# Attention block of four 512-channel images on one core: batches written out one after the other, ScalarE sets the scores' starting values for every step, maxima in units of 256 and 512 keys

## The chip, the cores and the metric

The kernel runs on one core of a Trainium2 chip. The metric is the device time of one execution in microseconds (us). Before the change three runs gave 4076.78, 4077.01 and 4074.82 us, median 4076.78.

## What is computed

The reference is a group norm, eight-head attention over the 48 x 48 positions of an image, a projection, and the normalised input added back. Four images (batches) of 512 channels, T = 2304 positions, heads of 64 channels, all in fp32:

```
xn  = groupnorm(x, 32 groups) * gn_w + gn_b              # (4, 512, 2304)
q, k, v = split(qkv_w @ xn + qkv_b)                      # 8 heads of 64 channels
w   = softmax(q^T k / sqrt(64))                          # 2304 x 2304 per head
a   = v w^T
out = xn + proj_w @ a + proj_b
```

## The kernel before, in words

Two heads (a pair) are worked on together, each in one half of TensorE's 128 rows or columns. A batch has 4 pairs. A pair's queries are cut into 6 chunks of N = 384, its keys into 18 tiles of 128. A **step** is one key tile for one query chunk, both heads: scores of 128 keys x 384 queries per head, `Exp` on ScalarE (L756) into one of 8 ring places in `probs`, the product with the values on TensorE (`make_pv`, L577), and on GpSimd the addition into `denom` (L1087), 17 additions for the 18 steps of a chunk. Two steps make a **slot**; 9 slots make a block (one query chunk of a pair), 54 slots a pair, 216 slots a batch, 864 slots the kernel.

Before `Exp`, the scores must be lowered by each query's maximum. `max_unit` (L517) computes scores roughly, for 128 queries and one chunk of 384 keys, both heads, into `aux_banks`; VectorE takes the maximum of each (L864); when a block's queries are complete the maxima are negated (L869), transposed (L877), sent through DRAM (`neg_rows`) and read back over all partitions as `seeds`. This runs 24 steps ahead. The accurate scores of a step are three products (high parts, low part of keys, low part of queries, L557) added to the negated maximum already in the bank. In even steps ScalarE copies `seeds` into the bank (L769); in odd steps TensorE multiplies a matrix of 1/64 (`shares`) with `seeds` (L553).

TensorE's order inside a slot is written out:

```
unit_of_step(first); make_scores(first); make_scores(second); unit_of_step(second)
[pieces of projections of q, k, v for the next pair]   # before[i]
make_pv(first - 2); make_pv(first - 1)
[finish of a block: sum of denom over partitions]      # after[i]
```

There is one `aux_banks`: a unit waits until VectorE has taken the maxima of the unit before (`aux_done`). On ScalarE the order of a slot is `Exp`, `Exp`, seed of the next even step, then the high parts of q and k (L716), values (L720) or saving of the output sums (L741). VectorE takes the unit's maxima, pieces of the reciprocal of the sums (L945 to L961), and the low parts of q and k (L857), which wait for the high part. In the first three pairs of a batch (inner pairs) the projections for the next pair are cut into pieces: in each block three of them, and they end in slots 1, 5 and 8 of the block. Twelve of the eighteen in a pair are of q or k. In the last pair they are whole, and VectorE takes the next batch's statistics (slots 0 to 11), a short chain of small operations gives its coefficients (slots 14 to 16), and ScalarE normalises it (L736, slots 16 to 27).

When a batch's stream of slots ends, TensorE computes the last block's sums (L534) once GpSimd has finished, and then the projection (L656): six chunks of 384 positions, each 48 matmuls. Its input `att` is read back from DRAM into two buffers `att_in`, and split into a high part (ScalarE, L747, into the key buffers) and a low part (VectorE, L967, in place). ScalarE adds the bias into `proj_sb`, VectorE adds the normalised input to it in `xres` (L1022), both in the ring `probs`; SyncE stores `xres` and loads the input for the chunk after next into it. The next batch's first seed on ScalarE waits until the stores have landed. Every engine runs the first three batches as a loop (`Fori`), the fourth written out behind it.

Of the kernel before, what the change touches and what calls it, by code (L numbers as in the profile page):

```python
# [5 lines left out]
def attention_block_program(nc, x, gn_w, gn_b, wqkv_t, bqk, bv, wproj_t, bproj, att, out):  # L6
# [39 lines left out]
    AHEAD = KT + 6  # L46
    EARLY_Q = 2
# [13 lines left out]
    NORM_AT, NORM_EVERY = 33, 2  # L61

# [101 lines left out]
    with ExitStack() as ctx:  # L164
# [10 lines left out]
        seeds = [sb(f"seeds{i}", [128, 2 * N], fp32r) for i in range(2)]  # L175
        shares = sb("shares", [128, 128], fp32r)
# [15 lines left out]
        att_in = [sb(f"att_in{i}", [128, CT, N], fp32r) for i in range(2)]  # L192
# [3 lines left out]
        neg_max = sb("neg_max", [128, 32], fp32r)  # L196
# [3 lines left out]
        spare = sb("spare", [128, 1])  # L200
        small = sb("small", [128, 64])
# [12 lines left out]

        def head(e):
            return slice(e * D, (e + 1) * D)
# [9 lines left out]

        def xres(i):
            return probs[:, CT * N * i:CT * N * (i + 1)].rearrange("p (o n) -> p o n", n=N)

        proj_sb = probs[:, 2 * CT * N:4 * CT * N].rearrange("p (o n) -> p o n", n=N)  # L230
        att_hi = [buf[:, 0:CT * N].rearrange("p (k n) -> p k n", n=N)
                  for buf in (k_hi[(PAIRS - 1) % 2], k_lo[(PAIRS - 1) % 2])]
# [62 lines left out]
        def first_batch(k):  # L295
            return isinstance(k, int)
# [40 lines left out]
        def _(sp):  # L337
# [15 lines left out]
            def send_max(n, blk):  # L353
# [8 lines left out]
                if not isinstance(n, int) or n >= 2:  # L362
                    sp.wait_ge(seeded, PRIMED + KT // 2 * (n - 1))
                    sp.wait_ge(probs_ready, PROBS_PRIMED + KT * (n - 1))
                sp.dma_start(seeds[par][:, :].bitcast(fp32), neg_rows.rearrange("r q -> (r q)").partition_broadcast(128))\
# [8 lines left out]
            def stream(b, last):  # L374
                before, _ = PLANS[last]
                nb = b + 1
                for s in range(BSTEPS):
# [18 lines left out]
                    if s in PUT_AT:  # L396
                        put_block(b, PUT_AT[s])
# [13 lines left out]
            def load_att(b, tc):  # L411
                i = tc % 2
                sp.dma_start(att_in[i][:, :, :].bitcast(fp32), att[:, :, chunk(tc)]
                             .rearrange("k c t -> c k t")).then_inc(att_back[i], 16)
# [4 lines left out]
            def projection(b):  # L419
                sp.wait_ge(att_out, PRIMED + 16 * (BLOCKS * b + BLOCKS - 1))  # L420
                load_att(b, 0)
                load_att(b, 1)
                put_block(b, BLOCKS - 1)

                for tc in range(2):
                    if tc == 1:
                        sp.wait_ge(att_out, PRIMED + 16 * BLOCKS * (b + 1))
# [36 lines left out]
            with sp.Fori(0, B - 1) as b:  # L464
                batch(b, False)
            batch(B - 1, True)
# [11 lines left out]
        def _(pe):  # L478
            mm = nc.tensor.matmul

            def bank_for(u):

                if not isinstance(u[1], int) or u[1] > 0:
                    pe.wait_ge(bank_free[u[0]], u[1])
                return bank(u)
# [26 lines left out]
            def max_unit(n, p, qt, kc):  # L512

                if not isinstance(n, int) or n > 0:
# [23 lines left out]
            def make_scores(s, b):  # L538


# [4 lines left out]
                if s % 2 == 0:  # L545
                    pe.wait_ge(seeded, PRIMED + BSTEPS // 2 * b + s // 2 + 1)
                else:
                    if s >= 2:
                        pe.wait_ge(probs_ready, PROBS_PRIMED + BSTEPS * b + s - 1)
                    if kt == 1:  # L550
                        pe.wait_ge(seeds_in[blk % 2], 16 * (BLOCKS // 2 * b + blk // 2 + 1))
                    for e in range(2):
                        mm(slot[:, e, :], shares[head(e), :], seeds[blk % 2][head(e), e * N:(e + 1) * N],  # L553
                           start=True, stop=False)
                for n, (ks, qs) in enumerate(((k_hi[par], q_hi), (k_lo[par], q_hi), (k_hi[par], q_lo))):
                    for e in range(2):
                        last = mm(slot[:, e, :], ks[head(e), keys], qs[head(e), queries],  # L557
                                  start=False, stop=(n == 2), skip_group_check=(s % 2 == 0))
                last.then_inc(scores_full, 1)

            def open_banks():

                for e in range(2):
                    last = mm(scores[:, 0, e, 0:N], k_hi[0][head(e), 0:128], q_hi[head(e), chunk(0)],
                              start=True, stop=True)
# [53 lines left out]
            def stream(b, last):  # L619
# [17 lines left out]
                finish(b, BLOCKS - 1, use(b, last, TAIL))  # L637
                if not last:
                    wait_free(pe, use(b, last, ("v", PAIRS, VG - 1)))

            def projection(b):

                pe.wait_ge(wproj_lo_ready, 1)
                for tc in range(CH):
                    i = tc % 2
                    for low in range(2):
                        pe.wait_ge(att_lo_ready if low else att_hi_ready, CH * b + tc + 1)
                        products = ([(wproj_hi, att_in[i])] if low
                                    else [(wproj_hi, att_hi[i]), (wproj_lo, att_hi[i])])
                        for ot in range(CT):  # L650
# [3 lines left out]
                            for w, a in products:  # L654
                                for k in range(CT):
                                    last = mm(scores[:, n // 2 % 2, n % 2, 0:N], w[:, k, ot * 128:(ot + 1) * 128],  # L656
# [489 lines left out]
```

## Time and profile before

| | |
|---|---|
| median of three runs | 4076.78 us |
| profiled execution, device time | 4077.72 us |
| its span, first to last instruction | 4076.0 us |
| mean granted TensorE clock | 0.988 of full |
| TensorE busy | 3933.8 us, 97% |
| GpSimd busy | 3004.5 us, 74% |
| ScalarE busy | 2308.0 us, 57% |
| VectorE busy | 2217.9 us, 54% |

Busy is the time in which at least one instruction of the engine ran. TensorE's instructions overlap: two matmuls, one in each half of the array, start together, and the next two start before they have ended, so that the distance between starts and not the duration is what one costs. Shares are means over the whole span: the stream of slots, the last pair of a batch and the projection have to be read apart.

### The profile page before, as it was taken

Reading aid. Unit: us, or ns where it says so; the run is one execution under the profiler, and the core shown is the slowest. Engines: PE = TensorE matmul, PEld = TensorE weight load, DVE = VectorE, ACT = ScalarE, POOL = GpSimd, SP = SyncE. Lnnn points to the kernel's source line nnn. Section 1 sums busy time; section 2 is a strip of 40 time slices with the busy share of each in tenths; the row PEclk is TensorE's granted clock in tenths of the full one; section 3 lists DMA queues with packets and bytes.
Section 4 is the critical chain, followed back from the end, with each engine's and each line's share of the span. In section 5 each row is a group of like instructions: output and inputs, shape, how many; then the busy total and the mean of one; then the engine's idle time right before and its main releaser. Section 6 shows DMA issues by size and latency. Waiting matters only on the chain.

```text
span 4076.0 us, 84658 instructions
## 1 busy us (share of the span) xinstructions
PE 3933.8 (97%) x31730; PEld 2472.5 (61%) x31730; DVE 2217.9 (54%) x2809; ACT 2308.0 (57%) x3159; POOL 3004.5 (74%) x1639
## 2 busy tenths in 40 slices
PE   6999999999899999999989999999999999999997
PEld 3566665656656566565665656566567565656656
DVE  4555555565455555566545555556644555555552
ACT  2555555565455555556535555555654555555563
POOL 0778878777288888877728888887773888888893
PEclk9999999999999999999999999999999999999999
DMA  2000000120400000012130000002113000000004
GB/s 74 16 20 24 18 22 21 43 87 18 148 19 18 22 22 20 20 57 73 39 131 18 22 21 16 24 20 75 59 43 121 21 16 21 22 18 19 19 19 144
DMA packets 133751, 165.87 MB, mean 41 GB/s; under 512 B 61648, under 2 KB 110800, under 8 KB 132816
## 3 DMA queue, kind: packets, MB, share of 16 engines
q1 hardware_dynamic: 133328, 160.26, 12.5%
q8 instruction: 262, 4.29, 0.4%
q14 instruction: 161, 1.32, 0.1%
HBM read 122.17 MB, written 38.04 MB: 39 GB/s over the span
## 4 chain that ended last, share of the span: by engine, by line
PE 88%; issue 4%; DVE 3%; POOL 3%; DMA 2%; SPq 0%; ACT 0%; POOLq 0%; DVEq 0%; ACTq 0%
PE oacc L577 26%; PE scores L557 20%; PE pool_bank L495 13%; PE aux_banks L517 13%; PE pool_bank L507 7%; PE scores L656 3%; PE scores L553 3%; POOL denom L1087 3%; PE pool_bank L534 2%; DMA att_in<-att 1%; DVE maxima L864 1%; DVE turned L945 1%; DMA out<-probs 1%; PE scores L495 1%; PE scores L507 0%
## 5 line engine op out<-in xcount | busy, mean ns | idle before, releaser
L1087 POOL TENSOR_TENSOR denom<-denom,probs 128x768 f32<-128x768 f32 x1536 | 2829.3, 1842 | 568.3 <-ACT probs L756 473.3
L864 DVE TENSOR_REDUCE maxima<-aux_banks 128x2 f32<-128x768 f32 x1728 | 1657.2, 959 | 1389.1 <-PE aux_banks L517 1379.4
L756 ACT ACTIVATE probs<-scores 128x768 f32<-128x768 f32 x1728 | 1347.2, 812 | 1259.2 <-PE scores L557 1253.2
L577 PE MATMUL oacc<-probs,vals 128*64 128x384 f32 x6912 | 1277.0, 491 | 0.0
L517 PE MATMUL aux_banks<-k_hi,q_hi 64*128 64x384 f32 x3456 | 762.5, 437 | 43.2 <-DVE maxima L864 39.2
L577 PEld LDWEIGHTS oacc<-probs,vals 128*64 128x64 f32 x6912 | 471.1, 137 | 503.9 <-issue 466.8
L517 PEld LDWEIGHTS aux_banks<-k_hi,q_hi 64*128 64x128 f32 x3456 | 323.2, 184 | 693.2 <-issue 451.2
L769 ACT ACTIVATE scores<-seeds 128x768 f32<-128x768 f32 x864 | 700.1, 810 | 4.3 <-DMA out<-probs 4.3
L557 PE MATMUL scores<-q_hi,k_hi 64*128 64x384 f32 x3456 | 587.3, 335 | 22.7 <-ACT scores L769 22.6
L557 PE MATMUL scores<-q_lo,k_hi 64*128 64x384 f32 x3456 | 588.6, 335 | 0.0
L557 PE MATMUL scores<-q_hi,k_lo 64*128 64x384 f32 x3456 | 585.6, 334 | 0.0
L1084 POOL TENSOR_TENSOR denom<-probs 128x768 f32<-128x768 f32 x96 | 174.6, 1819 | 442.1 <-ACT probs L756 442.1
L557 PEld LDWEIGHTS scores<-q_hi,k_hi 64*128 64x128 f32 x3456 | 327.4, 186 | 33.9 <-ACT scores L769 32.7
L557 PEld LDWEIGHTS scores<-q_lo,k_hi 64*128 64x128 f32 x3456 | 328.0, 185 | 0.0
L557 PEld LDWEIGHTS scores<-q_hi,k_lo 64*128 64x128 f32 x3456 | 327.3, 185 | 0.0
L495 PE MATMUL pool_bank<-xn,wq 128*64 128x384 f32 x1504 | 293.2, 505 | 1.6
L553 PE MATMUL scores<-seeds,shares 64*128 64x384 f32 x1728 | 292.7, 334 | 0.0
L507 PE MATMUL pool_bank<-wv,xn 128*64 128x128 f32 x4416 | 287.9, 277 | 1.8
L495 PE MATMUL pool_bank<-xn,wk 128*64 128x384 f32 x1456 | 281.4, 501 | 1.9
L507 PEld LDWEIGHTS pool_bank<-wv,xn 128*64 128x64 f32 x4416 | 236.9, 137 | 42.9 <-issue 36.6
L553 PEld LDWEIGHTS scores<-seeds,shares 64*128 64x128 f32 x1728 | 163.2, 185 | 0.0
L495 PEld LDWEIGHTS pool_bank<-xn,wq 128*64 128x64 f32 x1504 | 90.1, 137 | 103.1 <-issue 96.8
(91 smaller groups left out, 1681.3 us busy)
## 6 DMA issues: line engine op xcount, KB each, us to landing
seeds<-neg_rows SPq DMA_DIRECT2D x96, 384.0 KB, 3.5
xtile<-x SPq DMA_DIRECT2D x72, 384.0 KB, 3.2
att<-o_norm SPq DMA_DIRECT2D x96, 192.0 KB, 1.9
att_in<-att SPq DMA_DIRECT2D x24, 768.0 KB, 6.3
probs<-x SPq DMA_DIRECT2D x24, 768.0 KB, 4.7
out<-probs SPq DMA_DIRECT2D x24, 768.0 KB, 5.2
neg_rows<-neg_cols SPq DMA_DIRECT2D x384, 0.8 KB
xn<-x SPq DMA_DIRECT2D x4, 1152.0 KB, 8.6
```

Of the source, the lines that this page charges most:

```text
L495: last = mm(to[head(e), 0:N], w[:, k, head(e)], xn[:, k, chunk(c)], start=(k == 0), stop=(k == CT - 1))
L507: last = mm(to[head(half), i * 128:(i + 1) * 128], xn[:, k, t0:t0 + D], wv[:, k, :], start=(k == 0), stop=(k == CT - 1))
L517: last = mm(aux_banks[:, e, 0:N], q_hi[head(e), qt * 128:(qt + 1) * 128], k_hi[p % 2][head(e), chunk(kc)], start=True, stop=True)
L553: mm(slot[:, e, :], shares[head(e), :], seeds[blk % 2][head(e), e * N:(e + 1) * N], start=True, stop=False)
L557: last = mm(slot[:, e, :], ks[head(e), keys], qs[head(e), queries], start=False, stop=(n == 2), skip_group_check=(s % 2 == 0))
L577: ins = mm(oacc[head(e), 0:N], vals[p % 2][:, kt, head(e)], prob(s)[:, e * N:(e + 1) * N], start=(kt == 0), stop=(kt == KT - 1))
L656: last = mm(scores[:, n // 2 % 2, n % 2, 0:N], w[:, k, ot * 128:(ot + 1) * 128], a[:, k, :], start=(not low and w is wproj_hi and k == 0), ...
L756: a(prob(s).rearrange("p (h n) -> p h n", n=N), scores[:, s % 2, :, 0:N], ACT.Exp, scale=SCALE).then_inc(probs_ready, 1)
L769: a(scores[:, 0, :, 0:N], seeds[blk % 2][:, :].bitcast(fp32).rearrange("p (e n) -> p e n", n=N), ACT.Copy).then_inc(seeded, 1)
L864: v.tensor_reduce(maxima[:, :, qt, kc], aux_banks[:, :, 0:N], AX.X, ALU.max).then_inc(aux_done, 1)
L1084: gp.tensor_tensor(acc, prob(s - 1), prob(s), ALU.add).then_inc(added, 1)
L1087: gp.tensor_tensor(acc, acc, prob(s), ALU.add).then_inc(added, 1)
```

## The change

Four things are changed.

1. The loops over batches are gone; each engine's program has all four batches one behind the other.
2. Seeds: ScalarE copies the negated maxima into the bank for all steps. Its order in a slot becomes `Exp(s)`, `seed(s+2)`, `Exp(s+1)`, `seed(s+3)`; a seed waits for the `Exp` just before it. TensorE's products with `shares` go.
3. Maxima units: the six units of 384 keys become three pairs of 256 and 512 keys. The unit at the head of a slot is of 256, the second of 512.
4. The end of a batch: the attention output has buffers of its own for raw, high and low part. The chunks 0 and 1 are loaded during block 20 and later of the last pair, chunk 2 after block 22; the high and low part of chunk 0 are made in four pieces in slots 43 to 47 of the last pair. The last block's sums are computed after the first chunk of the projection instead of ahead of it. `xres` and `proj_sb` change places in the ring, and wait for GpSimd accordingly. The next batch's seeds 0 and 1 are written by ScalarE between the last copies of the projection, and it waits for the stores only at step 4.

```diff
+    UNIT_KEYS = (256, 512)
+    SPLIT_AT = 43
-            with pe.Fori(0, B - 1) as b:
-                batch(b, False)
-            batch(B - 1, True)
+            for b in range(B):
+                batch(b, b == B - 1)
...
             def max_unit(n, p, qt, kc):
...
-                    last = mm(aux_banks[:, e, 0:N], q_hi[head(e), qt * 128:(qt + 1) * 128],
-                              k_hi[p % 2][head(e), chunk(kc)], start=True, stop=True)
+                    last = mm(aux_banks[:, e, 0:UNIT_KEYS[kc % 2]], q_hi[head(e), qt * 128:(qt + 1) * 128],
+                              k_hi[p % 2][head(e), unit_keys(kc)], start=True, stop=True)
...
             def make_scores(s, b):
-                if s % 2 == 0:
-                    pe.wait_ge(seeded, PRIMED + BSTEPS // 2 * b + s // 2 + 1)
-                else:
-                    if s >= 2:
-                        pe.wait_ge(probs_ready, PROBS_PRIMED + BSTEPS * b + s - 1)
-                    if kt == 1:
-                        pe.wait_ge(seeds_in[blk % 2], 16 * (BLOCKS // 2 * b + blk // 2 + 1))
-                    for e in range(2):
-                        mm(slot[:, e, :], shares[head(e), :], seeds[blk % 2][head(e), e * N:(e + 1) * N],
-                           start=True, stop=False)
+                pe.wait_ge(seeded, PRIMED + BSTEPS * b + s + 1)
...
                 make_pv(BSTEPS - 1, b, last)
-                finish(b, BLOCKS - 1, use(b, last, TAIL))
...
+            def projection(b, last):
                 for tc in range(CH):
+                    if tc == 1:
+                        finish(b, BLOCKS - 1, use(b, last, TAIL))
...
             def exponentials(s, b):
+                if s == 0:
+                    act.wait_ge(out_ready, PRIMED + PJ * b)
+                if s == RING // 2:
+                    for i in range(2):
+                        act.wait_ge(stored[i], PRIMED + 16 * (CH // 2) * b)
...
             def stream(b, last):                       # ScalarE
-                seed(0, b)
                 for i in range(PAIRS * SLOTS):
                     for s in range(GS * i, GS * i + GS):
                         exponentials(s, b)
-                    if GS * i + 2 < BSTEPS:
-                        seed(GS * i + 2, b)
+                        if s + 2 < BSTEPS:
+                            seed(s + 2, b)
...
+                    n = i - (PAIRS - 1) * SLOTS - SPLIT_AT
+                    if 0 <= n < CT:
+                        att_high(b, 0, slice(n, n + 1))
-                att_high(b, 0)
...
             def projection(b, last):                   # ScalarE
+                    if n == PJ - 3 and not last:
+                        seed(0, b + 1, PRIMED + PJ * b + n + 1)
+                    if n == PJ - 1 and not last:
+                        seed(1, b + 1, PRIMED + PJ * b + n + 1)
...
             def projection(b):                         # SyncE
-                    if tc + 2 < CH:
-                        sp.wait_ge(proj_full, PJ * b + CT * (tc + 1))
-                        load_att(b, tc + 2)
+                    if tc + 3 < CH:
+                        load_next_att(b, tc + 1)       # waits for att_lo_ready of chunk tc + 1
```

## Rows read from the trace of the kernel before

**Rows 1.** The page's chain that ended last, shares of the span by engine

```profile
PE 88%; issue 4%; DVE 3%; POOL 3%; DMA 2%; SPq 0%; ACT 0%; POOLq 0%; DVEq 0%; ACTq 0%
```

**Rows 2.** The page's groups: line, engine, tiles, count | busy us, mean ns | idle before, releaser

```profile
L1087 POOL TENSOR_TENSOR denom<-denom,probs 128x768 f32<-128x768 f32 x1536 | 2829.3, 1842 | 568.3 <-ACT probs L756 473.3
L864 DVE TENSOR_REDUCE maxima<-aux_banks 128x2 f32<-128x768 f32 x1728 | 1657.2, 959 | 1389.1 <-PE aux_banks L517 1379.4
L756 ACT ACTIVATE probs<-scores 128x768 f32<-128x768 f32 x1728 | 1347.2, 812 | 1259.2 <-PE scores L557 1253.2
L769 ACT ACTIVATE scores<-seeds 128x768 f32<-128x768 f32 x864 | 700.1, 810 | 4.3 <-DMA out<-probs 4.3
L553 PE MATMUL scores<-seeds,shares 64*128 64x384 f32 x1728 | 292.7, 334 | 0.0
```

**Rows 3.** Timeline of an inner-pair slot that ends a projection (start us, us, engine, line)

```profile
1472.32 0.34 PE L557 MATMUL scores<-q_hi,k_hi 64*128 64x384 f32 x2
...
1473.54 0.44 PE L517 MATMUL aux_banks<-k_hi,q_hi 64*128 64x384 f32 x2
...
1473.91 1.51 PE L495 MATMUL pool_bank<-xn,wq 128*64 128x384 f32 x8
...
1474.53 0.81 ACT L769 ACTIVATE scores<-seeds 128x768 f32<-128x768 f32 x1
...
1475.46 0.58 ACT L716 ACTIVATE q_hi<-pool_bank,bias_q 128x384 fp32r<-128x384 f32 x1
...
1476.08 0.62 DVE L857 SCALAR_TENSOR_TENSOR q_lo<-pool_bank,bias_q,q_hi 128x384 fp32r<-128x384 f32 x1 [0.53 <-ACT q_hi L716]
1476.64 0.44 PE L517 MATMUL aux_banks<-k_hi,q_hi 64*128 64x384 f32 x2
1477.12 0.96 DVE L864 TENSOR_REDUCE maxima<-aux_banks 128x2 f32<-128x768 f32 x1 [0.43 <-PE aux_banks L517]
```

**Rows 4.** Timeline of a slot with no projection, in the last pair of batch 0

```profile
901.71 0.44 PE L517 MATMUL aux_banks<-k_hi,q_hi 64*128 64x384 f32 x2
...
903.41 1.02 ACT L736 ACTIVATE xn<-xtile,small 128x768 f32<-128x768 f32 x1
903.52 0.44 PE L517 MATMUL aux_banks<-k_hi,q_hi 64*128 64x384 f32 x2
903.80 0.34 PE L557 MATMUL scores<-q_hi,k_hi 64*128 64x384 f32 x2
...
904.53 1.57 ACT L756 ACTIVATE probs<-scores 128x768 f32<-128x768 f32 x2
...
905.02 0.44 PE L517 MATMUL aux_banks<-k_hi,q_hi 64*128 64x384 f32 x2
...
905.99 0.81 ACT L769 ACTIVATE scores<-seeds 128x768 f32<-128x768 f32 x1
```

**Rows 5.** Chain of waits within 3900 to 4000 us, by line

```profile
by line: POOL denom L1087 68.3%; PE oacc L577 8.6%; PE scores L557 7.6%; issue 4.7%; PE aux_banks L517 3.9%; ACT probs L756 2.3%; PE pool_bank L534 2.2%; POOL denom L1084 1.8%; PE scores L553 0.9%; POOLq L1086 0.6%; ACTq L755 0.1%; POOLq L1
```

**Rows 6.** Timeline at the coefficients of the next batch (slot 16 of the last pair)

```profile
867.25 0.69 PE L517 MATMUL aux_banks<-k_hi,q_hi 64*128 64x384 f32 x2 [5.64 <-DVE maxima L864]
```

**Rows 7.** Timeline from the end of batch 0's stream to batch 1's

```profile
1033.09 2.80 PE L577 MATMUL oacc<-probs,vals 128*64 128x384 f32 x16
...
1040.28 1.55 PE L534 MATMUL pool_bank<-denom,ones 128*64 128x384 f32 x4 [4.38 <-POOL denom L1087]
...
1098.27 0.44 PE L517 MATMUL aux_banks<-k_hi,q_hi 64*128 64x384 f32 x2 [0.94 <-ACT probs L814]
...
1103.98 1.28 ACT L769 ACT_TABLE_LOAD   x1 [6.04 <-DMA out<-probs]
...
1106.14 0.69 PE L557 MATMUL scores<-q_hi,k_hi 64*128 64x384 f32 x2 [7.43 <-ACT scores L769]
```

**Rows 8.** Chain of waits in order of time: one chunk of the projection (start, us, what)

```profile
1088.72 8.63 PE scores L656 x48
```

**Rows 9.** Timeline at the end of the last batch

```profile
4015.84 1.55 PE L534 MATMUL pool_bank<-denom,ones 128*64 128x384 f32 x4 [12.13 <-POOL denom L1087]
```

**Rows 10.** Busy time by windows: stretch, us, engines' busy us, granted clock, DMA share, GB/s

```profile
1031.50:1106.00 74.50, 59.10 (x328) 54.41 (x326) 30.03 (x39) 25.41 (x35) 8.41 (x4) 0.92 0.57 190
4004.00:4076.00 72.00, 54.65 (x292) 52.35 (x292) 26.37 (x34) 20.22 (x30) 11.07 (x6) 0.89 0.53 178
```

More of the change, by code:

```diff
@@ L174, in attention_block_program @@
         k_lo = [sb(f"k_lo{i}", [128, T], fp32r) for i in range(2)]
-        seeds = [sb(f"seeds{i}", [128, 2 * N], fp32r) for i in range(2)]
-        shares = sb("shares", [128, 128], fp32r)
+        seeds = [sb(f"seeds{i}", [128, 2 * N]) for i in range(2)]
         xn = sb("xn", [128, CT, T])
@@ L191, in attention_block_program @@
         wproj_lo = sb("wproj_lo", [128, CT, C], fp32r)
-        att_in = [sb(f"att_in{i}", [128, CT, N], fp32r) for i in range(2)]
+        att_hi0 = sb("att_hi0", [128, CT, N], fp32r)
+        att_lo0 = sb("att_lo0", [128, CT, N], fp32r)
+        att_raw1 = sb("att_raw1", [128, CT, N])
         groups = sb("groups", [128, 128])
@@ L213, in chunk, with unit_keys @@
             return slice(c * N, (c + 1) * N)
+        def unit_keys(kc):
+            start = kc // 2 * sum(UNIT_KEYS) + kc % 2 * UNIT_KEYS[0]
+            return slice(start, start + UNIT_KEYS[kc % 2])
         def head(e):
@@ L295, in first_batch @@
         def first_batch(k):
[L296 removed]
+            return k == 0
         def wait_full(engine, u):
@@ L557, in make_scores @@
                         last = mm(slot[:, e, :], ks[head(e), keys], qs[head(e), queries],
-                                  start=False, stop=(n == 2), skip_group_check=(s % 2 == 0))
+                                  start=False, stop=(n == 2), skip_group_check=True)
                 last.then_inc(scores_full, 1)
             def open_banks():
-                for e in range(2):
-                    last = mm(scores[:, 0, e, 0:N], k_hi[0][head(e), 0:128], q_hi[head(e), chunk(0)],
-                              start=True, stop=True)
+                for slot in range(2):
+                    for e in range(2):
+                        last = mm(scores[:, slot, e, 0:N], k_hi[0][head(e), 0:128], q_hi[head(e), chunk(0)],
+                                  start=True, stop=True)
                 last.then_inc(banks_opened, 1)
@@ L655, in projection @@
                                 for k in range(CT):
-                                    last = mm(scores[:, n // 2 % 2, n % 2, 0:N], w[:, k, ot * 128:(ot + 1) * 128],
-                                              a[:, k, :], start=(not low and w is wproj_hi and k == 0),
-                                              stop=(low == 1 and k == CT - 1))
+                                    ins = mm(scores[:, n // 2 % 2, n % 2, 0:N], w[:, k, ot * 128:(ot + 1) * 128],
+                                             a[:, k, :], start=(not low and w is wproj_hi and k == 0),
+                                             stop=(low == 1 and k == CT - 1))
                             if low:
-                                last.then_inc(proj_full, 1)
+                                ins.then_inc(proj_full, 1)
             pe.sem_inc(pv_done, PRIMED)
-            pe.wait_ge(consts_made, 5)
+            pe.wait_ge(consts_made, 4)
             units = 0
@@ L701, in batch @@
                 stream(b, last)
-                projection(b)
-            with pe.Fori(0, B - 1) as b:
-                batch(b, False)
-            batch(B - 1, True)
+                projection(b, last)
+            for b in range(B):
+                batch(b, b == B - 1)
         @block.scalar
@@ L757, in exponentials, with seed @@
                   scale=SCALE).then_inc(probs_ready, 1)
-            def seed(s, b):
+            def seed(s, b, since=None):
                 blk = s // KT
@@ L765, in seed @@
                     act.wait_ge(banks_opened, 1)
-                    act.wait_ge(proj_saved, PRIMED + PJ * b)
+                    act.wait_ge(proj_saved, since)
                 else:
                     act.wait_ge(probs_ready, PROBS_PRIMED + BSTEPS * b + s - 1)
-                a(scores[:, 0, :, 0:N], seeds[blk % 2][:, :].bitcast(fp32).rearrange("p (e n) -> p e n", n=N),
+                a(scores[:, s % 2, :, 0:N], seeds[blk % 2][:, :].rearrange("p (e n) -> p e n", n=N),
                   ACT.Copy).then_inc(seeded, 1)
@@ L838, in batch @@
             def batch(b, last):
-                for i in range(2):
-                    act.wait_ge(stored[i], PRIMED + 16 * (CH // 2) * b)
+                a(warm[:, :], ones[:, 0:1], ACT.Exp)
                 stream(b, last)
-                projection(b)
-            with act.Fori(0, B - 1) as b:
-                batch(b, False)
-            batch(B - 1, True)
+                projection(b, last)
+            act.wait_ge(consts_made, 4)
+            for s in range(2):
+                seed(s, 0, PRIMED)
+            for b in range(B):
+                batch(b, b == B - 1)
         @block.vector
@@ L1063, in batch @@
                 stream(b, last)
-                projection(b)
-            with dve.Fori(0, B - 1) as b:
-                batch(b, False)
-            batch(B - 1, True)
+                projection(b, last)
+            for b in range(B):
+                batch(b, b == B - 1)
         @block.gpsimd
@@ L1104, in batch @@
                     add(s, b)
-            with pool.Fori(0, B - 1) as b:
+            for b in range(B):
                 batch(b)
-            batch(B - 1)
 def kernel(**inputs):
```

98 lines of the change are left out of this document (58 added, 40 removed).

## The prediction

> **What bounds the kernel now.** I read the chain of waits first: 88% of it is TensorE [rows 1], so what comes off TensorE's own queue comes off the time, unless something else is then late. The groups [rows 2] say who could be late: GpSimd needs 17 x 1.842 = 31.3 us of additions for a block of nine slots, ScalarE 0.81 us for an `Exp` or a seed, VectorE 0.96 us for the maxima of a unit of 384 keys. Then I read the timeline by stage, because the shares mix them.
>
> In inner pairs a slot is TensorE's work end to end [rows 3]: scores at 1472.32, the second unit at 1473.54, the projection at 1473.91, the next slot's first unit at 1476.64. Seven pairs of matmuls fill the 1.22 us from scores to unit, 0.174 us each; durations of 0.33 us overlap. A slot with nothing extra has 3.31 us (units at 901.71 and 905.02 [rows 4]); a quarter of a projection, or the sum of a block, adds 0.65 and a half 1.29. An inner block has three half slots, which end a projection (4.60), and so 38.3 us, well above GpSimd's 31.3.
>
> The last pair of the last batch has no such filler; there the chain is GpSimd's [rows 5], 31.3 a block whatever TensorE does. Between batches TensorE stands: at 1035.9 (end of 1033.09 + 2.80) it waits 4.38 us for GpSimd, and after the projection its first scores come at 1106.14, 8 us after the unit at 1098.27, since the seed waited for the stores [rows 7]. The two windows [rows 10] show 15.4 and 17.4 us without a matmul and a granted clock of 0.92 and 0.89 of the 2.4 GHz level, so part of them ran at 1.2 GHz after the standstills.
>
> **Seeds: what goes.** 864 slots lose one pair of matmuls, 0.174 us each: the most that this can give is 150 us. In the last pair of the last batch GpSimd takes it back except in the four slots with a projection. In the other 15 pairs it is what hides behind it that counts.
>
> **Seeds: what comes.** ScalarE now does four operations a slot, with a seed that waits for the end of the `Exp` before it. From rows 4: the `Exp` starts 0.73 us after its scores (903.80 to 904.53); two `Exp` and the start of the seed behind them take 1.46 us, 0.73 to 0.75 each, as neighbours overlap. A waiting seed can't overlap: I take 0.81 + 0.04 = 0.85. Bounds for this: 0.74 if the wait costs nothing, 1.1 if it costs as much again as the 0.28 us between a unit and the scores behind it; the value is near the lower end because VectorE's instruction behind a ScalarE result starts 0.04 us after it (1475.46 + 0.58 to 1476.08). The group of four then has 0.85 + 0.75 + 0.85 + 0.75 = 3.2 us to the start of what follows, where it was 2.2 for three.
>
> (a) *Slots that end a projection of q or k.* Scores at 0; `Exp` at 0.73; high part at 0.73 + 3.2 = 3.93 instead of 3.14 (1475.46 less 1472.32); low part on VectorE 0.62 later, at 4.55, done 5.17. The next slot starts at 4.60 - 0.17 = 4.43; its first unit is issued at 4.20 and full at 4.63, where VectorE had been free for 0.43 us [rows 3]; now it is busy until 5.17. The unit's maxima (0.69, below) end at 5.86, and the second unit, due at 4.43 + 6 x 0.174 = 5.47, starts at about 5.9. TensorE loses 0.42 us, behind a queue in order: everything of the slot is behind that unit. 12 projections in a pair x 12 inner pairs = 144 times: **+60 us**. Bounds: 0.2 us each if the group is 2.98 us long (all four overlap), 0.8 if each seed costs 0.2 more: +29 to +115.
> (b) *Slots without filler.* The loop is: scores full and `Exp` at 0.73, second seed done 3.26 later, 0.06 to the matmul, then 2.61 us of TensorE (3.14 less 0.52) to the next but one slot's scores. It goes over two slots: (0.73 + 3.26 + 0.06 + 2.61)/2 = 3.33 us. So these slots gain nothing against 3.31, whereas TensorE alone would have 3.14. With a quarter of a projection the loop is (0.73 + 3.26 + 0.06 + 3.79 - 0.52)/2 = 3.66, less than TensorE's 3.79: hidden. They are some 23 in each of three last pairs.
> (c) *Normalisation in the last pair.* 1.02 us more on ScalarE a slot [rows 4]: 3.2 + 1.02 = 4.2 us in slots 16 to 27, seven of which have 3.3 to 4.0. Slots 17 to 20 give +2.4, 23, 24 and 27 together +1.3; the coefficients' chain [rows 6] starts some 0.8 later. About +4.5 a batch, +1 for the split of `att`, against -4.3 for 25 filled slots: net +2 each, **+6** for three batches (0 to +20).
>
> The Trainium skill's page "ScalarE: Activation LUTs" (What ACT_TABLE_LOAD costs) says that ACTIVATEs back to back overlap by about 93 ns; rows 4 show 0.05 to 0.08. If that held for the waiting seeds too, it would be the lower bound of (a), 31 us less than the sum. Its page "Perfetto Trace Analysis" (step T11) says that a semaphore is seen only after the write is acknowledged, which speaks for the 0.85.
>
> **Maxima units.** Same columns on TensorE in a slot (256 + 512 = 768). One rate from 959 ns for 768 values, bounded by no fixed part (0.64 and 1.28) and by a fixed part of a third (0.75 and 1.17): I take 0.69 and 1.23. Without this the second unit would come late: unit to maxima 0.48, 0.96, release 0.05 = 1.49, just the 0.28 + 1.22 that TensorE takes now; the seeds' pair gone, all would be lost again. With 256 keys it is 0.43 + 0.69 + 0.05 = 1.17 against 1.27: hidden. The second: 0.53 + 1.23 + 0.05 = 1.81 against 1.81 in a slot without filler, more otherwise: just hidden. In slots 3 and 4 of a block the transposes (0.11 of wait now) get room: **-5**. Whether a pair of 256 columns is really cheaper than 0.174 no row shows; if weight loads set that pace the longer unit adds 0.05 us a slot, up to +46.
>
> **The gain of the inner pairs** is 648 x 0.174 = **-113**, and the sum of the stream -113 + 60 - 5 + 6 = -52.
>
> **End of a batch.** From the last slot's scores (1031.5) to the next batch's (1106.1) there are 74.6 us. After: 4.2 to the end of the stream, six chunks of 8.4 (8.63 less the overlap [rows 8]), the sum 0.8, 0.3 to the scores: 55.7. The 4.4 us of GpSimd's lag (perhaps 6.5 now) lie behind the first chunk; reads of `att` and `x` are a chunk ahead (a store and the load behind it take about 11 us of the 16.8 between two uses of a buffer). Seed 1 comes only after the last copy, +1.3 in the first slot, about what the 1.2 GHz costs there now. 18.5 x 3 = **-55**; bounds -25 (reads late as now) to -60. The last batch: from GpSimd's end (4015.84 [rows 9], fixed by GpSimd relative to the stream) sum, five chunks instead of six and the same tail: 60.2 to about 49, **-11** (-4 if 3.8 us of standstill bring the clock down).
>
> **Straight program.** Two or three loop ends go, inside the boundary above. Nothing else: 0.
>
> **Sum.** -52 - 55 - 11 = -118 on the profiled execution of 4077.7 (span 4076.0, 1.7 around it): 3960; the median of the runs is 0.9 lower: 3959 us.
>
> **Rivals.**
> A. *The cover holds*: high parts come early enough. Then (a) is about 5 and (b) gives 10 more: 3959 - 55 - 10 = 3894 us. For it: in rows 3 VectorE has 0.43 us of room. Against: ScalarE's group grows by 1.0.
> B. *ScalarE is somewhat slower*: 0.2 more per waiting seed. (a) 0.8 each, +55; (b) +0.2 on 69 slots, +14: 4028 us.
> C. *Slower than before*: the same loop on ScalarE, if a waiting seed costs c more than my 0.85. (a) grows by 2c x 144, (b) by c x 69: it cancels 118 us from c = 0.33 on; at 0.4 it is +143: 4102 us. For: every slot has two such waits and no row shows one on ScalarE. Against: 0.04 us between engines.
> D. *The batch ends give half*, because `xres` is now loaded only after GpSimd's end and SyncE's queue is in order: +30: 3989 us.
>
> **Chances.** Forecast 0.47, A 0.18, B 0.15, D 0.14, C 0.06. A measurement tells about 0.2% (8 us) from no change. Faster 0.93, same 0.02, slower 0.05. The range that leaves out most of C and the ends of A and B: 3893 to 4035.
>
> **What would show it.** Blocks 0 to 3 of an inner pair at 38.0 us (38.3 now), blocks 4 and 5, which have only values, at 36.8: the difference is (a), and the second unit in slots 2, 6 and 0 waits for L864. L716 at 3.9 us behind the slot's scores. Filler-free slots at 3.33. First scores of the next batch 56 us after the last slot's, no drop of the clock there. The forecast is wrong if the value-only blocks don't go to 36.8 (then ScalarE or the units' width bounds), or if L553's 150 us come off whole.

## The result, and the profile after

The changed kernel takes 3943.1 us (median of four runs, 3941.5 to 3945.0) against 4076.9: a ratio of 0.9671, 95% interval 0.9654 to 0.9688. The profiled execution has a span of 3940.3 us against 4076.0, so 135.7 us have to be accounted for. The forecast was 3959 us.

The page's chain by engine and the groups that answer to [rows 1, 2] (line numbers have moved: L896 is the maxima, L780 `Exp`, L793 the seed, L544 the unit on TensorE, L574 the scores; further down, L734 and L889 are high and low part):

```profile
PE 69%; ACT 16%; issue 6%; DVE 6%; POOL 2%; SPq 1%; DMA 0%; ACTq 0%; POOLq 0%; DVEq 0%
...
L896 DVE TENSOR_REDUCE maxima<-aux_banks 128x2 f32<-128x512 f32 x1728 | 1655.0, 958 | 1204.1 <-PE aux_banks L544 1184.1
L780 ACT ACTIVATE probs<-scores 128x768 f32<-128x768 f32 x1728 | 1385.3, 802 | 510.9 <-PE scores L574 500.6
L793 ACT ACTIVATE scores<-seeds 128x768 f32<-128x768 f32 x1728 | 1408.6, 815 | 79.4 <-PE scores L582 10.0
L544 PE MATMUL aux_banks<-k_hi,q_hi 64*128 64x512 f32 (+1 forms) x3456 | 705.8, 404 | 88.7 <-DVE maxima L896 82.8
```

TensorE holds 69% of the chain where it held 88%; 16% have gone to ScalarE and 6% are VectorE's. So the next microsecond is to be had elsewhere than in TensorE's queue alone. The sum of VectorE's maxima is unchanged (1655.0 us), only divided otherwise.

Where the time went, from the first scores matmul of each slot in both traces:

| stretch | before | after | difference | forecast |
|---|---|---|---|---|
| start to first scores | 101.3 | 99.3 | -2.0 | 0 |
| 12 inner pairs, sum | 2763.6 | 2683.8 | -79.8 | -58 |
| last pairs of batches 0 to 2, sum | 714.9 | 723.9 | +9.0 | +6 |
| last pair of batch 3 | 197.5 | 197.7 | +0.2 | 0 |
| three batch ends, last scores to first scores | 222.2 | 170.9 | -51.3 | -55 |
| last scores to the end | 76.5 | 64.7 | -11.8 | -11 |

**The slot.** The timeline of an inner slot that ends a q projection, start and duration in us, against [rows 3]:

```profile
1299.37 0.81 ACT L780 ACTIVATE probs<-scores 128x768 f32<-128x768 f32 x1 [0.42 <-POOL denom L1117]
...
1300.21 0.81 ACT L793 ACTIVATE scores<-seeds 128x768 f32<-128x768 f32 x1
...
1300.96 0.79 ACT L780 ACTIVATE probs<-scores 128x768 f32<-128x768 f32 x1
...
1301.79 0.82 ACT L793 ACTIVATE scores<-seeds 128x768 f32<-128x768 f32 x1
...
1302.54 0.57 ACT L734 ACTIVATE q_hi<-pool_bank,bias_q 128x384 fp32r<-128x384 f32 x1
...
1303.14 0.62 DVE L889 SCALAR_TENSOR_TENSOR q_lo<-pool_bank,bias_q,q_hi 128x384 fp32r<-128x384 f32 x1 [1.86 <-ACT q_hi L734]
...
1303.67 0.68 DVE L896 TENSOR_REDUCE maxima<-aux_banks 128x2 f32<-128x512 f32 x1
...
1304.41 0.50 PE L544 MATMUL aux_banks<-k_hi,q_hi 64*128 64x512 f32 x2 [0.30 <-DVE maxima L896]
```

Read it from below: the second unit (1304.41) waits for the first unit's maxima; those began at 1303.67, as the low part was ending; the low part waited 1.86 us for the high part; and the high part began 3.17 us after the slot's first `Exp`, behind four operations. The slot's scores began at 1298.56, so the high part came 3.98 us after them.

**The batch end.** Timeline from batch 0 to batch 1, against [rows 7]:

```profile
1016.35 2.80 PE L595 MATMUL oacc<-probs,vals 128*64 128x384 f32 x16
...
1019.08 0.96 PE L675 MATMUL scores<-att_hi,wproj_hi 128*128 128x384 f32 x4
...
1027.60 0.87 PE L561 MATMUL pool_bank<-denom,ones 128*64 128x384 f32 x4
...
1071.47 0.39 PE L544 MATMUL aux_banks<-k_hi,q_hi 64*128 64x256 f32 x2 [1.18 <-ACT probs L841]
...
1071.69 0.34 PE L574 MATMUL scores<-q_hi,k_hi 64*128 64x384 f32 x2
```

The projection starts where the stream ends, the block's sum stands behind the first chunk without a wait, and the next scores follow the unit by 0.22 us, not 8. The windows that answer to [rows 10] (us, busy us of TensorE, its loads, VectorE, ScalarE, GpSimd, granted clock, DMA share, GB/s) show 1.2 us without a matmul and a granted clock of 1.00, the 2.4 GHz level, in the first, and 0.97 at the end of the kernel:

```profile
1014.70:1071.70 57.00, 55.82 (x328) 52.36 (x328) 27.07 (x35) 24.47 (x35) 10.24 (x5) 1.00 0.61 198
...
3880.00:3940.30 60.30, 52.98 (x294) 51.64 (x292) 26.09 (x33) 21.34 (x30) 10.11 (x5) 0.97 0.62 200
```

### The profile page after: what moved, and what is told of

Its sections match the earlier page's. It is cut to its first block, busy times and chain, and to the rows that moved or that the text cites. A ratio compares the mean times of both kernels' runs of the same rounds, so it can differ in the third digit from the quotient of the medians.

```text
span 3940.3 us, 74532 instructions
## 1 busy us (share of the span) xinstructions
PE 3776.6 (96%) x30004; PEld 2262.9 (57%) x30004; DVE 2221.4 (56%) x2820; ACT 3066.5 (78%) x4037; POOL 3003.3 (76%) x1639
## 3 DMA queue, kind: packets, MB, share of 16 engines
q8 instruction: 237, 3.88, 0.4%
## 4 chain that ended last, share of the span: by engine, by line
PE 69%; ACT 16%; issue 6%; DVE 6%; POOL 2%; SPq 1%; DMA 0%; ACTq 0%; POOLq 0%; DVEq 0%
PE oacc L595 21%; PE scores L574 15%; PE aux_banks L544 10%; ACT probs L780 9%; PE pool_bank L522 8%; PE pool_bank L534 7%; PE scores L675 5%; ACT scores L793 5%; DVE maxima L896 3%; POOL denom L1120 2%; PE pool_bank L561 1%; ACT k_hi L734 1%; ACT q_hi L734 1%; DVE k_lo L889 1%; DVE q_lo L889 1%
## 5 line engine op out<-in xcount | busy, mean ns | idle before, releaser
L896 DVE TENSOR_REDUCE maxima<-aux_banks 128x2 f32<-128x512 f32 x1728 | 1655.0, 958 | 1204.1 <-PE aux_banks L544 1184.1
L780 ACT ACTIVATE probs<-scores 128x768 f32<-128x768 f32 x1728 | 1385.3, 802 | 510.9 <-PE scores L574 500.6
L793 ACT ACTIVATE scores<-seeds 128x768 f32<-128x768 f32 x1728 | 1408.6, 815 | 79.4 <-PE scores L582 10.0
L544 PE MATMUL aux_banks<-k_hi,q_hi 64*128 64x512 f32 (+1 forms) x3456 | 705.8, 404 | 88.7 <-DVE maxima L896 82.8
L544 PEld LDWEIGHTS aux_banks<-k_hi,q_hi 64*128 64x128 f32 x3456 | 324.2, 184 | 705.7 <-issue 450.8
L574 PE MATMUL scores<-q_hi,k_hi 64*128 64x384 f32 x3456 | 602.6, 345 | 36.6 <-ACT scores L793 34.0
L574 PE MATMUL scores<-q_lo,k_hi 64*128 64x384 f32 x3456 | 587.3, 335 | 0.0
L574 PE MATMUL scores<-q_hi,k_lo 64*128 64x384 f32 x3456 | 586.8, 335 | 0.0
L574 PEld LDWEIGHTS scores<-q_hi,k_hi 64*128 64x128 f32 x3456 | 327.2, 186 | 91.5 <-ACT scores L793 84.5
L574 PEld LDWEIGHTS scores<-q_hi,k_lo 64*128 64x128 f32 x3456 | 327.6, 186 | 0.0
L574 PEld LDWEIGHTS scores<-q_lo,k_hi 64*128 64x128 f32 x3456 | 326.8, 185 | 0.0
L841 ACT ACTIVATE probs<-scores,small 128x384 f32<-128x384 f32 x96 | 55.5, 581 | 123.2 <-PE scores L675 97.6
L522 PEld LDWEIGHTS pool_bank<-xn,wk 128*64 128x64 f32 x1456 | 87.7, 135 | 110.7 <-issue 105.3
```

Source lines behind the costliest of these rows:

```text
L522: last = mm(to[head(e), 0:N], w[:, k, head(e)], xn[:, k, chunk(c)], start=(k == 0), stop=(k == CT - 1))
L544: last = mm(aux_banks[:, e, 0:UNIT_KEYS[kc % 2]], q_hi[head(e), qt * 128:(qt + 1) * 128], k_hi[p % 2][head(e), unit_keys(kc)], start=True, ...
L780: a(prob(s).rearrange("p (h n) -> p h n", n=N), scores[:, s % 2, :, 0:N], ACT.Exp, scale=SCALE).then_inc(probs_ready, 1)
L793: a(scores[:, s % 2, :, 0:N], seeds[blk % 2][:, :].rearrange("p (e n) -> p e n", n=N), ACT.Copy).then_inc(seeded, 1)
L896: v.tensor_reduce(maxima[:, :, qt, kc], aux_banks[:, :, 0:UNIT_KEYS[kc % 2]], AX.X, ALU.max)\
```

## The experiments

Two things were open. First, the inner pairs gained 80 us and not 58: the slots without a low part's wait fell by 0.26 us (3.96 to 3.70), though the removed pair of matmuls is 0.174. Second, whether the wait behind the low part is really caused by ScalarE's order. My theory for the first: before, the second unit came just when VectorE let it go, 1.49 us after the first; I had called that a tie that costs nothing, but a unit that has to wait, however little, can't have its weights loaded behind the matmul ahead.

**Seeds and widths apart.** Three kernels complete a square. `e1_units384`:

```diff
-    UNIT_KEYS = (256, 512)
+    UNIT_KEYS = (384, 384)
```

> The changed kernel with all maxima units of 384 keys again; the rest as changed. Theory A (the second unit's wait for VectorE is what the widths remove, and with it a weight load of 0.11 us that could not be made ahead): the second unit comes 1.49 us after the first, as before, so slots keep the old lengths (3.96 us with a quarter projection, not 3.70), and the 12 slots of a pair behind a low part wait some 0.4 us: an inner pair has about 235 us instead of 224, and the run about 4075 us. Theory B (the whole gain of the slots is TensorE's removed products, the widths only cover it a little): an inner pair stays under 227 us, the run under 3985 us.

`e3_pe_seeds`:

```diff
-                pe.wait_ge(seeded, PRIMED + BSTEPS * b + s + 1)
+                if s % 2 == 0:
+                    pe.wait_ge(seeded, PRIMED + BSTEPS // 2 * b + s // 2 + 1)
+                else:
+                    ...                                   # waits as in the kernel before
+                    for e in range(2):
+                        mm(slot[:, e, :], shares[head(e), :], seeds[blk % 2][head(e), e * N:(e + 1) * N], ...)
```

> The changed kernel with the odd steps' starting values made by TensorE again (matrix of 1/64 times seeds); units of 256 and 512 keys, the end of the batch and the straight program stay. Theory A (widths are worth some 0.09 us in each slot by themselves, and ScalarE's four operations cost the 0.58 us waits behind the low parts): slots with a quarter projection 3.87 us, no wait behind the low parts, an inner pair 225 us, last pairs of batches 0 to 2 some 5 us shorter than in the changed kernel; about 3940 us, level with the changed kernel. Theory B (the widths give only 5 us in all): an inner pair 230 us, 4005 us.

In `e3` ScalarE's order is also the old one again, `Exp`, `Exp` and one seed a slot. `e4_pe_seeds_384` has both edits.

> Odd starting values on TensorE and units of 384 keys: of the change only the straight program and the new end of a batch are left. Both theories: inner pairs 230 us as before, 57 us instead of 74 from a batch's last scores to the next batch's first, the last batch's tail 12 us shorter: about 4012 us. A rival: if the changed stream had also hidden part of the end, it is above 4025.

| median us (ratio to before, 95% interval) | units of 384 | units of 256 and 512 |
|---|---|---|
| odd seeds on TensorE | 4015.1 (0.9843, 0.9826 to 0.9859) | 3935.4 (0.9648, 0.9632 to 0.9665) |
| all seeds on ScalarE | 4081.7 (1.0008, 0.9999 to 1.0018) | 3943.1 (0.9671, 0.9654 to 0.9688) |

`e1` and `e3` land where theory A had them (4075 and 3940), far from B (under 3985, and 4005). So:

- The widths alone are worth 80 us, and 139 with the seeds on ScalarE. They are the larger part of the stream's gain, where I had put 5 us. The prediction had said that without them the seeds' gain "would be lost again", and it is: with units of 384 and the seeds on ScalarE (`e1`) the inner pairs take 2815 us, 51 more than before. It had not seen that they gain where the seeds' products stay.
- The seeds on ScalarE cost 67 us with units of 384 and are level, 8 us worse by the medians, with 256 and 512 (the two intervals overlap). In this form, the step gives nothing.
- The end of the batch and the straight program are the first cell: 4015.1, some 62 us. In its trace the inner pairs have 230.3 us, as before, and a batch end 57.0 to 57.3, so the changed stream hides nothing of the end.

**How a wait of nearly nothing costs 0.1 us.** `e12_units320`:

```diff
-    UNIT_KEYS = (256, 512)
+    UNIT_KEYS = (320, 448)
```

> The changed kernel with maxima units of 320 and 448 keys. Theory A (it is not only the length of the wait that counts: as soon as the second unit waits for VectorE at all, its weight load of 0.11 us is no longer made behind the matmul ahead of it): the first unit's maxima are taken 1.31 us after its start against 1.30 us that TensorE needs, so the wait itself is 0.01 to 0.05 us but slots get some 0.1 us longer; value blocks go from 36.4 to about 37.4, inner pairs from 224 to about 230, the run to 4000 to 4015 us. Rival (only the wait itself counts): under 0.05 us a slot, the run under 3975 us.

4002.8 us (0.9817, 0.9802 to 0.9832), inner pairs 229 us: theory A. A slot with a quarter of v has 3.82 to 3.84 us against 3.70. Three traces show the second unit's load; before the change, the changed kernel, `e12` (PEld is the weight load, PE the matmul):

```profile
1473.54 0.18 PEld L517 LDWEIGHTS aux_banks<-k_hi,q_hi 64*128 64x128 f32 x2
```

```profile
1250.74 0.19 PEld L544 LDWEIGHTS aux_banks<-k_hi,q_hi 64*128 64x128 f32 x2
...
1250.84 0.41 PE L544 MATMUL aux_banks<-k_hi,q_hi 64*128 64x512 f32 x2
...
1251.17 0.88 PE L534 MATMUL pool_bank<-wv,xn 128*64 128x128 f32 x12
```

```profile
1251.15 0.83 DVE L896 TENSOR_REDUCE maxima<-aux_banks 128x2 f32<-128x640 f32 x1 [1.34 <-PE aux_banks L544]
1252.03 0.19 PEld L544 LDWEIGHTS aux_banks<-k_hi,q_hi 64*128 64x128 f32 x2 [0.19 <-DVE maxima L896]
1252.03 0.47 PE L544 MATMUL aux_banks<-k_hi,q_hi 64*128 64x448 f32 x2
```

Before, load and matmul both start at 1473.54 (the matmul in [rows 3]), and the next matmuls come 0.37 us later. After, the load starts 0.10 ahead of the matmul and what follows comes 0.33 later, although the unit has 512 keys and not 384. In `e12` the maxima end at 1251.98 and load and matmul start together again.

This is so throughout. Of the 648 slots of the inner pairs, the second unit's load starts less than 0.03 us ahead of its matmul in 644 before, 642 in `e12` and 647 in `e1`, but in 173 of the changed kernel and in 4 of `e3`. Where the load is ahead, a unit costs TensorE 0.22, 0.25, 0.28 and 0.33 us to the next matmul for 256, 320, 384 and 512 keys; where it is not, 0.37, 0.40 and 0.43 us for 384, 448 and 512. So the 0.26 us of a slot are 0.16 for the seeds' pair (1.22 to 1.06 us from scores to second unit), 0.06 for the first unit (0.28 to 0.22) and 0.04 for the second (0.37 to 0.33).

The waits' totals hint at it (who waited for whom: idle us of the load's queue in total, which need not be lost on TensorE, times, longest), for the kernel before, the changed one, `e12` and `e1`:

```profile
PEld aux_banks L517 <- DVE maxima L864: 196.7, 658, 6.0
```

```profile
PEld aux_banks L544 <- DVE maxima L896: 212.6, 315, 5.5
```

```profile
PEld aux_banks L544 <- DVE maxima L896: 310.0, 872, 3.9
```

```profile
PEld aux_banks L544 <- DVE maxima L896: 387.5, 876, 3.8
```

It is 658 times in the kernel before, a row that I had not used: it says that the load was late in most slots, though not what that costs. It is on the load, not the matmul (whose own waits for the maxima were 39.2 us, 29 times), and so easily passed over.

**The low part's wait.** `e6_high_first`, ScalarE:

```diff
                         exponentials(s, b)
+                        if s % GS == GS - 1:
+                            for key in completed(before[i]):
+                                if key[0] in "qk":
+                                    behind(key, b, last)      # the high part
                         if s + 2 < BSTEPS:
                             seed(s + 2, b)
...                                                           # behind the seeds: values only
```

> The changed kernel, but ScalarE makes the high part of q or k ahead of the slot's last seed instead of behind it. Theory A (VectorE's low part is late because ScalarE's high part stands behind a fourth operation, and the second unit of the next slot pays 0.5 to 0.7 us, 144 times): the waits go, inner pairs 217 us instead of 224, 3860 us. Rival (those waits come from the longer maxima of 512 keys or from GpSimd): under 20 us gained, 3925 or more.

3870.8 us (0.9482, 0.9466 to 0.9497), 11 above what theory A gave and far from the rival's 3925. Inner pairs have 217.9 us, as forecast to 1 us. The timeline of `e6` behind such a slot, with 0.22 us to spare for VectorE and the unit in time:

```profile
1275.74 0.62 DVE L894 SCALAR_TENSOR_TENSOR q_lo<-pool_bank,bias_q,q_hi 128x384 fp32r<-128x384 f32 x1 [0.98 <-ACT q_hi L734]
1276.15 0.39 PE L544 MATMUL aux_banks<-k_hi,q_hi 64*128 64x256 f32 x2
1276.58 0.69 DVE L901 TENSOR_REDUCE maxima<-aux_banks 128x2 f32<-128x512 f32 x1 [0.22 <-PE aux_banks L544]
1277.43 0.40 PE L544 MATMUL aux_banks<-k_hi,q_hi 64*128 64x512 f32 x2
```

Slot by slot, against the changed kernel, slots 2, 6 and 0 behind a low part give back 84 us in the inner pairs; 71 are left in the sum, mainly because slot 5 of a block gets 11 us longer. In it the second unit is still late, in value blocks of the changed kernel too: 4.63 us for the 4.36 of a like slot. VectorE is in the product that normalises the last block's output (L994, here L999) when the first unit comes due, so that the maxima begin only as it ends (`e6`, read from the timeline, not tested):

```profile
1177.53 1.67 DVE L999 TENSOR_TENSOR o_norm<-o_raw,recip 128x384 f32<-128x384 f32 x1
...
1179.12 0.68 DVE L901 TENSOR_REDUCE maxima<-aux_banks 128x2 f32<-128x512 f32 x1
...
1179.85 0.50 PE L544 MATMUL aux_banks<-k_hi,q_hi 64*128 64x512 f32 x2
```

The slot's scores began at 1178.58, so the second unit came 1.27 us after them and not 1.06. Over the 72 blocks of the inner pairs this is some 20 us in `e6`, and the fastest version below still has it.

`e7_low_later` treats the same wait at its other end, on VectorE: the low part is held until the next slot's first unit has had its maxima.

```diff
                         unit_of_step(s, b, last)
+                        for key in held:
+                            behind(key, b, last)
+                        held = []
...
                     for key in completed(before[i]):
-                        behind(key, b, last)
+                        held.append(key)                      # q and k only
```

> The changed kernel, but VectorE makes the low part of q or k after the maxima of the next slot's first unit instead of ahead of them. Theory A: the second unit no longer waits; what is left is up to 0.15 us where the next projection's first piece waits for the bank: 3865 us. Rival as for the run before: 3925 us or more.

3890.3 us (0.9529, 0.9513 to 0.9545): the wait goes, 0.18 us of it come back where the next projection waits for the bank (4.52 and 3.88 in slots 0 and 6 where `e6` has 4.34 and 3.70), which makes the pairs 219.3. It is 20 us above `e6`, 19 of them in the inner pairs (2632.0 against 2612.6). My 3865 was 5 us above what I expected of `e6`: I had counted the bank's wait far too low.

**The waiting seed.** `e8_exp_exp`, ScalarE:

```diff
                     for s in range(GS * i, GS * i + GS):
                         exponentials(s, b)
+                    for s in range(GS * i, GS * i + GS):
                         if s + 2 < BSTEPS:
                             seed(s + 2, b)
```

> The changed kernel with ScalarE's order Exp, Exp, seed, seed in a slot, so that no seed waits for the Exp right before it. Theory A (a waiting seed costs 0.1 us each because it can't overlap): the group of four is 0.2 us shorter, high parts come 0.2 earlier, 144 x 0.2 = 29 us less, and slots without filler fall from 3.36 to about 3.2: 3905 us. Rival (a waiting seed costs nothing, or the first seed is now the late one for the next slot's first scores): 3943 us or more.

3874.8 us (0.9491, 0.9475 to 0.9506), 30 us better than expected. A slot that ends a q projection in `e8`:

```profile
1276.57 1.51 ACT L780 ACTIVATE probs<-scores 128x768 f32<-128x768 f32 x2 [0.43 <-PE scores L574]
...
1277.97 1.55 ACT L793 ACTIVATE scores<-seeds 128x768 f32<-128x768 f32 x2
1279.44 0.58 ACT L734 ACTIVATE q_hi<-pool_bank,bias_q 128x384 fp32r<-128x384 f32 x1
```

`Exp` to high part is 2.87 us, against 3.17 in the changed kernel: 0.30 for the two waits, 0.15 each, where I had expected 0.1. Inner pairs fall from 224 to 220, together 45 us, and last pairs of batches 0 to 2 from 241 to 234, together 22 us of the 68.

**The batch end.** `e10_finish_first`:

```diff
-                    if tc == 1:
+                    if tc == 0:
                         finish(b, BLOCKS - 1, use(b, last, TAIL))
```

> The changed kernel with the last block's sums ahead of the first chunk of the projection again. Theory A (the chunk hides GpSimd's lag): per batch end GpSimd's lag of about 6 us and the time at the 1.2 GHz level after it come back, 8 us x 3, and 8 to 12 in the last batch: 3975 us. Rival (the end is bound by the reads and stores, which don't change): 3943 to 3950 us.

3983.7 us (0.9759, 0.9742 to 0.9775), 41 more than the changed kernel. TensorE stands 6.3 us and works on at the 1.2 GHz level: the granted clock is 0.50 from 1026.7 to 1030 us, and four matmuls take 1.54 and 1.65 us (0.87 and 0.96 in the changed kernel):

```profile
1026.72 1.54 PE L561 MATMUL pool_bank<-denom,ones 128*64 128x384 f32 x4 [6.33 <-issue]
...
1028.20 1.65 PE L675 MATMUL scores<-att_hi,wproj_hi 128*128 128x384 f32 x4
```

From last to first scores it takes 65.9 us instead of 57.0, three times 8.9; the tail has 76.1 instead of 64.7. So of the 62 us of the ends, some 38 are this one move. The other 24 (own buffers for `att`, the early seeds, the straight program) were not taken apart but for the run that follows.

`e5_straight` is the kernel before with `for b in range(B)` in the place of `Fori` on all engines.

> The kernel before with its batches written out, nothing else. Theory A: the gap between the batches is the wait for the stores, 1.3 us of table load may go: 4072 to 4077 us. Rival: loop ends (instruction fetch behind a taken branch) hold a good part of the 17 us a batch end lost: 4050 or less.

4072.2 us (0.9987, 0.9977 to 0.9997): 6 us by the medians, 1 to 9 by the interval. The distance between batches is still 71 to 73 us, so the wait for the stores is not the loop's; the first seed still waits for them, only the table load of [rows 7] is not there:

```profile
1100.22 0.81 ACT L767 ACTIVATE scores<-seeds 128x768 f32<-128x768 f32 x1 [4.98 <-DMA out<-probs]
```

Something else changes with the loop. In inner pairs of the kernel before, the first `Exp` of a slot comes 0.73 us after its scores and the second 0.76 behind the first in the three batches of the loop, but 0.81 and 0.71 in the fourth, which was already written out. `e5` has 0.81 and 0.71 in all four. Why is not shown.

**Both orders together.** `e11_interleaved`, ScalarE's order `Exp`, `Exp`, seed, high part, seed:

```diff
                     for s in range(GS * i, GS * i + GS):
                         exponentials(s, b)
+                    for s in range(GS * i, GS * i + GS):
+                        if s % GS == GS - 1:
+                            for key in completed(before[i]):
+                                if key[0] in "qk":
+                                    behind(key, b, last)
                         if s + 2 < BSTEPS:
                             seed(s + 2, b)
...                                                           # behind the seeds: values only
```

> The changed kernel with ScalarE's order Exp, Exp, seed, high part of q or k, seed: the two orders tried before together. If what each gave is of different places (the high part's order the waits behind the low parts, 217.9 us in an inner pair; the two Exp together the last pairs, 234 us instead of 242), the run has 3848 us. Rival (each gave the same thing in another way): not under 3868 us.

3852.7 us (0.9447, 0.9434 to 0.9460), inner pairs 218.0, last pairs 234: the two gains are of different places, and this is the fastest version, 90 us below the changed kernel. Against `e3`, with the same widths and the same ends, the seeds on ScalarE pay 83 us here, after 65 in `e6` and 61 in `e8`.

## Why the prediction was right, and where it was not

*TensorE as the bound, and GpSimd in the last pair*: right. The last pair of batch 3 has 197.7 us against 197.5.

*The gain of a slot, 0.174*: the term that was mis-sized. It is 0.26 in value slots, and 151 us over the inner pairs without the low parts' waits (their sum is 2612.6 in `e6`), where 113 + 5 were forecast. 648 times 0.26 would be 168; slot 5 of each block keeps some 21 of them back. The removed matmuls are about as priced (0.16 to 0.17). The rest is the weight load above: that the second unit came "just" when TensorE was ready for it was right on the timing, and wrong in taking a tie for free. The 256 and 512 keys were entered as cover and -5 us; they are worth 80 on their own. The -5 was to come from the transposes in slots 3 and 4, and did not: slot 3 fell by no more than the others.

*Maxima of 0.69 and 1.23 us*: measured 0.69 and 1.23. The bound of +46 us, for the case that a pair of 256 columns costs as much as one of 384, is off: from unit to scores are 0.22 us, where it was 0.28.

*ScalarE's group, 3.2 us, and the low part*: right in place and mechanism. 3.17 us, high part at 3.98 (3.93 forecast), slots 2, 6 and 0 behind it longer by 0.55, 0.5 and 0.7 us, of which 0.1 is the load that is exposed. `e6` puts the cost at 2683.8 - 2612.6 = 71 us; 60 was forecast. The late second unit comes when it was forecast (5.85 us after the scores of the slot ahead, for 5.9); what differs is that it is due sooner, 5.40 in `e6` and not 5.47, and that its load is exposed on top. The first `Exp` comes 0.81 us after its scores and not 0.73. The row at 1299.37 puts it down to GpSimd, but it is 0.81 where the scores are waited for too, and in `e5`: the 0.73 of [rows 4] is that of a batch in the loop.

*Slots without filler*: two of them in a row take 3.05 and 3.65, 3.35 on average; 3.33 was forecast, by a loop that closes over two slots, and the alternation shows that it does.

*The last pairs of batches 0 to 2*: +9.0 against +6, the size right and the parts partly not. Normalisation cost less than forecast (slots 17 to 27: 49.7 us against 47.8, with the gain of the filled slots in it); the coefficients' stretch cost 4.7 us more in batch 0 and 3.4 in batch 1, where I had 0.8:

```profile
829.16 2.14 DVE L994 TENSOR_TENSOR o_norm<-o_raw,recip 128x384 f32<-128x384 f32 x1
...
833.83 0.79 PE L544 MATMUL aux_banks<-k_hi,q_hi 64*128 64x512 f32 x2 [2.72 <-DVE maxima L896]
```

A product of 1.4 us on the mean has 2.14 here and the coefficients' first links behind it; TensorE waits 2.72 us and then works in part at the 1.2 GHz level (granted clock 0.61 from 833.8 to 842 us). Why the product took 2.14 us was not tested.

*The batch ends*: 57.0 us for a forecast of 55.7. The sum had no term for the unit's wait for ScalarE's last copy, 1.18 us at 1071.47, though [rows 7] have it with 0.94. The first slot was held unchanged (+1.3 for the seed against the 1.2 GHz level); it went from 5.3 to 3.5 us on the mean of three batches, 5 us that stand with the inner pairs. The clock stays up as forecast.

*The last end*: -11.8 for -11. GpSimd's lag is 2 us longer than the first chunk:

```profile
3890.73 0.87 PE L561 MATMUL pool_bank<-denom,ones 128*64 128x384 f32 x4 [2.03 <-POOL denom L1120]
```

Of the rivals, A (the cover holds) is what `e6` had to build: 3871 us; its 3894 was too high for the same 0.1 us. B and C needed a waiting seed dearer than my 0.85 by 0.2 and 0.33 us; it is 0.84. (It is the seed that does not wait that is cheaper than I had it, 0.70 and not 0.75.) D wanted the ends at half; they gave 63 us of the 66. The 18 us of span that the forecast was too high are the larger gain of the slot (-33) against the dearer waits (+11), the last pairs and the ends (+3 each) and the start (-2). That they offset each other is luck, and so is one of the marks: blocks with only values were to have 36.8 us and have 37.1 and 36.4, although their slots gain 0.26 and not 0.174; the late unit in slot 5 and, in block 4, the low part ahead of it take the difference back. Blocks 1 to 3 have 37.8 for 38.0.

## What to carry to other kernels

When two engines hand a buffer back and forth and arrive together, there is still a price: the weight load of the waiting matmul moves into the open, about 0.1 us here in each slot, and the wait shows on the load's row, not on the matmul's. Here, moving work to an engine that is 57% busy gave nothing until that engine's order was changed, because what stood behind the new work (the high part) was what a third engine, and then the bound one, waited for: list the consumers of everything behind an inserted instruction, and let instructions that wait for the one just ahead of them stand one place further back. Where one engine lags at the end of a stage, put independent work of the next stage ahead of the wait.

## What the runs showed of the hardware

- A seed that waits for the `Exp` just ahead of it starts 0.84 us behind it (1299.37 to 1300.21); one that doesn't starts 0.70 behind (1276.57 to 1277.97 for two `Exp`). The wait costs the overlap, some 0.15 us, on an operation of 0.8 us.
- Two matmuls of 64 rows and 512 columns cost TensorE less in place, 0.33 us to the next (changed kernel), than two of 384 whose load was exposed, 0.37 (before); two of 384 whose load was ahead had 0.28.
- In batches run as a loop, the two `Exp` of a slot start 0.73 us after the scores and 0.76 behind each other; written out, 0.81 and 0.71 (the kernel before has both, `e5` the second alone).
- VectorE's maxima took 0.69, 0.83, 0.96, 1.09 and 1.23 us for 512, 640, 768, 896 and 1024 values: 0.27 us for each 256.
